# Exponents of the decays in the first stage: differences of running sums brought by a transfer, in place of two matmuls a chunk

## The reference

```python
weights = jnp.where(dist_matrix < CUTOFF, sens, 0.0)      # x = x + weights @ (norm(x) @ W + B)
...
dt = jax.nn.softplus(dt + dt_bias)
A = -jnp.exp(A_log)
dA = jnp.einsum('bclh,h->bhcl', dtc, A)
A_cum = jnp.cumsum(dA, axis=-1)
Lmat = jnp.exp(segsum(dA))                 # exp(cs[l] - cs[s]) for l >= s, else 0
Y_diag = jnp.einsum('bcln,bcsn,bhcls,bcshp->bclhp', Cc, Bc, Lmat, xdt)
decay_states = jnp.exp(A_cum[..., -1:] - A_cum)
states = jnp.einsum('bcln,bhcl,bclhp->bchpn', Bc, decay_states, xdt)
Y_off = jnp.einsum('bcln,bchpn,bhcl->bclhp', Cc, prevs, jnp.exp(A_cum))
Y = (Y_diag + Y_off + xh * D[:, None]).reshape(Bsz, L, D_INNER)
```

## Time and profile before

| what | us |
|---|---|
| median of 3 runs (2483.21 to 2485.96) | 2484.01 |
| the profiled execution | 2485.07 |
| its span, first to last instruction | 2483.2 |
| TensorE matmuls busy | 2268.9 |
| VectorE busy | 1940.7 |
| ScalarE busy | 1493.7 |
| GpSimd busy | 1173.4 |

### The profile page before, as it was taken

The page is one execution under the profiler, slowest core; times in us unless marked ns, Lnnn a source line. Parts: engine busy times, 40 slices in busy tenths (PEclk is TensorE's granted clock), DMA queues, the critical chain, the costliest instruction groups (busy, mean ns, idle before and its releaser), DMA issues.

```text
span 2483.2 us, 26160 instructions
## 1 busy us (share of the span) xinstructions
PE 2268.9 (91%) x8964; PEld 1414.8 (57%) x8964; DVE 1940.7 (78%) x2207; ACT 1493.7 (60%) x2208; POOL 1173.4 (47%) x906
## 2 busy tenths in 40 slices
PE   7998999999999999999899999999999997765998
PEld 4444555555555545545766676666666663433886
DVE  5677878787878776422899899999999898896765
ACT  4676666666667563324575756667675756663444
POOL 2102222223131314311987888888787888791000
PEclk9999999999999999999999999999999998687999
DMA  5232222222222222133323232332323221113121
GB/s 206 94 109 82 70 101 76 93 68 94 68 94 78 84 93 77 59 97 110 111 86 119 96 109 94 103 111 94 119 95 111 94 77 35 43 51 109 36 76 43
DMA packets 111445, 221.15 MB, mean 89 GB/s; under 512 B 7586, under 2 KB 65186, under 8 KB 110930
## 3 DMA queue, kind: packets, MB, share of 16 engines
q1 hardware_dynamic: 107106, 204.00, 25.4%
q0 software_dynamic: 3664, 14.45, 1.6%
q10 hardware_dynamic: 544, 1.05, 0.1%
HBM read 199.28 MB, written 20.19 MB: 88 GB/s over the span
## 4 chain that ended last, share of the span: by engine, by line
PE 42%; DVE 24%; issue 12%; POOL 12%; ACT 9%; DMA 0%; DVEq 0%; POOLq 0%; SPq 0%; ACTq 0%
PE ps L629 9%; POOL dB L2230 8%; DVE h L1431 5%; DVE wgt L1106 4%; PE ps L671 3%; DVE wgt L1099 3%; PE ps L798 2%; PE ps L920 2%; DVE acc L1403 2%; ACT ps L1618 2%; ACT th L1618 2%; POOL acc L2213 2%; PE ps L653 2%; PE ps L733 2%; POOL du L2226 2%
## 5 line engine op out<-in xcount | busy, mean ns | idle before, releaser
L2230 POOL TENSOR_TENSOR dB<-du,bc 128x512 f32<-128x512 f32 x512 | 656.2, 1299 | 92.2 <-DVE h L1431 88.7
L1431 DVE TENSOR_TENSOR_SCAN h<-ps,hst,dB 128x512 f32<-128x512 f32 x512 | 643.6, 1272 | 46.2 <-ACT ps L1618 35.2
L1618 ACT ACTIVATE ps<-dt,cols 128x512 f32<-128x512 f32 x512 | 351.4, 687 | 270.1 <-DVE h L1431 268.1
L629 PE MATMUL ps<-wgt,msg 128*128 128x512 f32 x1024 | 499.1, 596 | 15.1 <-DVE wgt L1106 13.6
L671 PE MATMUL ps<-raw,msg 128*128 128x256 f32 x1792 | 452.8, 389 | 0.9 <-ACT hb L1618 0.9
L920 PE MATMUL ps<-consts,h 128*128 128x128 f32 x2048 | 336.9, 292 | 97.7 <-DVE acc L1403 52.5
L920 PEld LDWEIGHTS ps<-consts,h 128*128 128x128 f32 x2048 | 257.5, 149 | 271.1 <-DVE acc L1403 110.3
L671 PEld LDWEIGHTS ps<-raw,msg 128*128 128x128 f32 x1792 | 331.8, 196 | 74.0 <-issue 39.3
L629 PEld LDWEIGHTS ps<-wgt,msg 128*128 128x128 f32 x1024 | 187.2, 191 | 219.6 <-issue 191.7
L1618 ACT ACTIVATE wgt<-wgt 128x1024 f32<-128x1024 f32 x256 | 258.4, 1049 | 56.1 <-DVE wgt L1099 54.5
L2213 POOL TENSOR_TENSOR acc<-acc,part 128x512 f32<-128x512 f32 x160 | 210.2, 1314 | 80.7 <-ACT part L1618 77.0
(11 more groups left out here) (320 smaller groups left out, 3559.0 us busy)
## 6 DMA issues: line engine op xcount, KB each, us to landing
raw<-in_adjT SPq DMA_DIRECT2D x256, 512.0 KB, 3.6
bc<-tmp_bc SPq DMA_DIRECT2D x64, 512.0 KB, 4.7
xb<-in_xT POOLq DMA_DIRECT2D x8, 512.0 KB, 4.1
tmp_x<-xb POOLq DMA_DIRECT2D x8, 512.0 KB, 3.1
x<-tmp_x SPq DMA_DIRECT2D x8, 512.0 KB, 4.8
tmp_x<-x SPq DMA_DIRECT2D x8, 512.0 KB, 3.6
raw<-tmp_xn SPq DMA_DIRECT2D x8, 512.0 KB, 4.0
tmp_xn<-x SPq DMA_DIRECT2D x7, 512.0 KB, 3.6
```

The source lines that it names most:

```text
L629: x = e.matmul(P[d][:, :], msg[:, j, d * 128:(d + 1) * 128], wgt[g % NW][:, l, :], start=j == 0, stop=j == NJ - 1)
L1431: e.tensor_tensor_scan(hr[n % 3][:, m, :], PS[4 + k % 2].t[:, :], dBr[k % 4][:, :], hst[:, n % 16, m:m + 1], ALU.mult, ALU.add).then_inc(S ...
L1618: return e.activation(out, in_, func, bias=bias, scale=scale)
L2230: e.tensor_tensor(dBr[k % 4][:, :], du[:, m, :], bcr[i % 3][:, n % 2, :], ALU.mult).then_inc(S("dB"), 1)
```

## The change

Running sums cs of dA now come once a block for all four chunks. They get a place in the ring of pre, behind z of the first tile: the three small matmuls that stood at the start of ssd, and a fourth, of dA as weights with tri, that gives the sums turned, 32 rows (chunk and head) of 128. ScalarE copies both out, to `sums_a` (two buffers) and `turned`; ecd is made from `sums_a`. GpSimd's queue stores `turned` to scratch memory, and one transfer a chunk (`load_sums`) brings the chunk's 8 rows to all 128 partitions, straight into E, which has three buffers. GpSimd subtracts the sums of the row's own position and takes the minimum with 0 (above the diagonal cs[l] - cs[s] is positive; cbm is 0 there), and ScalarE takes one exponential over 1024 in place. The load for the next chunk is issued behind the minimum of this one, the first of a block in step 38 of pre. rdA and its two matmuls are gone, and the rings are counted anew. The four steps of a chunk's inner part stay four.

Around it a few semaphores are joined (hst0 and zero1 with zero, A1exp with A1, sum0 with sum, so that the two sums over x3 at the end of a block of the second layer no longer wait for each other).

```diff
-        rdA = sb(cA, "rdA", [128, 8, 128])
-        E = [sb(cA, f"E{i}", [128, 8, 128]) for i in range(2)]
+        sums_a = [sb(cA, f"sums{i}", [128, 3, 4, 8]) for i in range(2)]
+        turned_a = sb(cA, "turned", [32, 128])
+        E = [sb(cA, f"E{i}", [128, 8, 128]) for i in range(3)]
...
-        pre_ring, ssd_ring = Ring(PS[2:4], 12 * NB), Ring(PS[4:8], 41 * NB)
+        pre_ring, ssd_ring = Ring(PS[2:4], 13 * NB), Ring(PS[4:8], 32 * NB)
...
+        def sums_use(ib):
+            return pre_use(ib, 5)
...
+                    if m == 0:
+
+                        b, dA = sums_use(ib), sms[p][:, 3, :]
+                        w.wait_ge(S("dA"), ib + 1)
+                        w.wait_ge(b.evac, b.n - 1)
+                        for k, x in enumerate((tri, trig, one)):
+                            e.matmul(b.ps[:, 32 * k:32 * k + 32], x, dA, start=True, stop=True)
+                        e.matmul(b.ps[0:32, 128:256], dA, tri, start=True, stop=True).then_inc(b.full, 1)
...
-                    yield from (None, None)
-                    for k in range(2):
-                        b = inner_use(ib, s, 2 + k)
-                        w.wait_ge(S("rdA"), 4 * ib + s + 1)
-                        w.wait_ge(b.evac, b.n - 1)
-                        e.matmul(b.ps[:, :], trig, rdA[:, 4 * k:4 * k + 4, :].rearrange("p h l -> p (h l)"),
-                                 start=True, stop=True).then_inc(b.full, 1)
-                        yield
+                    yield from [None] * 4
...
-                    xd, bn, Es, xdec = xdt[s % 2], bns[s % 2], E[s % 2], xdecs[s % 2]
+                    xd, bn, Es, xdec = xdt[s % 2], bns[s % 2], E[(4 * ib + s) % 3], xdecs[s % 2]
...
-                b = ssd_use(ib, 0)
-                w.wait_ge(S("dA"), ib + 1)
-                w.wait_ge(b.evac, b.n - 1)
-                for k, m in enumerate((tri, trig, one)):
-                    i = e.matmul(b.ps[:, 32 * k:32 * k + 32], m, dA, start=True, stop=True)
-                i.then_inc(b.full, 1)
...
-                    yield from (None, None)
+                    yield
+                    if m == 1:
+                        c = sums_use(ib)
+                        w.wait_ge(c.full, c.n)
+                        w.wait_ge(S("cut"), 8 * (ib - 1))
+                        w.wait_ge(S("d_turned"), 16 * ib)
+                        act(sums_a[p][:, :, :, :].rearrange("p a c h -> p (a c h)"), c.ps[:, 0:96], ACT.Identity).then_inc(S("sums_a"), 1)
+                        act(turned_a[:, :], c.ps[0:32, 128:256], ACT.Identity).then_inc(c.evac, 1)
+                    yield
...
-                    for k in range(2):
-                        b = inner_use(ib, s, 2 + k)
-                        w.wait_ge(b.full, b.n)
-                        if c >= 2:
-                            old = outer_use((c - 2) // 4, (c - 2) % 4, 2)
-                            w.wait_ge(old.full, old.n)
-                        act(E[s % 2][:, 4 * k:4 * k + 4, :].rearrange("p h l -> p (h l)"), b.ps[:, :], ACT.Exp).then_inc(b.evac, 1)
-                        yield
+                    x = E[c % 3][:, :, :].rearrange("p h l -> p (h l)")
+                    w.wait_ge(S("cut"), 2 * c + 2)
+                    act(x, x, ACT.Exp).then_inc(S("E"), 1)
+                    yield from (None, None)
...
-                b = ssd_use(ib, 0)
-                w.wait_ge(b.full, b.n)
+                w.wait_ge(S("sums_a"), ib + 1)
                 w.wait_ge(S("xdec"), 4 * ib)
                 w.wait_ge(S("hd"), 4 * ib)
                 if ib:
                     w.wait_ge(outer_use(ib - 1, 3, 0).evac, outer_use(ib - 1, 3, 0).n)
-                act(ecd[:, :, :, :].rearrange("p a c h -> p (a c h)"), b.ps[:, 0:96], ACT.Exp).then_inc(b.evac, 1)
+                act(ecd[:, :, :, :], sums_a[p][:, :, :, :], ACT.Exp).then_inc(S("ecd"), 1)
...
+            def load_sums(c):
+
+                if c >= 3:
+                    old = outer_use((c - 3) // 4, (c - 3) % 4, 2)
+                    w.wait_ge(old.full, old.n)
+                src = t["bc"][c // 4][2 * (c % 4):2 * (c % 4) + 2, :].rearrange("(o n) (a l) -> o (n a) l", o=1, l=128)
+                e.dma_start(E[c % 3][:, :, :], src.broadcast_to([128, 8, 128])).then_inc(S(f"d_E{c % 3}"), 16)
+
             def pre_a(ib):
-                yield from [None] * (NPA - 1)
+                yield from [None] * 24
+                b = sums_use(ib)
+                w.wait_ge(b.evac, b.n)
+                e.dma_start(t["bc"][ib][0:8, :].rearrange("n (a l) -> (n a) l", l=128), turned_a[:, :]).then_inc(S("d_turned"), 16)
+                yield from [None] * 14
+                w.wait_ge(S("d_turned"), 16 * (ib + 1))
+                load_sums(4 * ib)
+                yield from [None] * (NPA - 1 - 24 - 14)
...
-                    w.wait_ge(S("dA"), ib + 1)
-                    if c:
-                        old = inner_use((c - 1) // 4, (c - 1) % 4, 3)
-                        w.wait_ge(old.full, old.n)
-                    e.tensor_tensor(rdA[:, :, :], tri[:, None, :].broadcast_to([128, 8, 128]),
-                                    dA[:, 8 * s:8 * s + 8, None].broadcast_to([128, 8, 128]), ALU.mult).then_inc(S("rdA"), 1)
+
+                    x = E[c % 3][:, :, :]
+                    w.wait_ge(S("sums_a"), ib + 1)
+                    w.wait_ge(S(f"d_E{c % 3}"), 16 * (c // 3 + 1))
+                    e.tensor_tensor(x, x, sums_a[p][:, 0, s, :, None].broadcast_to([128, 8, 128]), ALU.subtract).then_inc(S("cut"), 1)
+                    w.wait_ge(S("cut"), 2 * c + 1)
+                    e.tensor_scalar(x, x, 0.0, None, ALU.min).then_inc(S("cut"), 1)
+                    if s < 3:
+                        load_sums(c + 1)
                     yield
                     w.wait_ge(X.evac, X.n)
-                    w.wait_ge(ssd_use(ib, 0).evac, ssd_use(ib, 0).n)
+                    w.wait_ge(S("ecd"), ib + 1)
                     if c >= 2:
                         old = outer_use((c - 2) // 4, (c - 2) % 4, 1)
                         w.wait_ge(old.full, old.n)
                     e.tensor_tensor(heads(xdec[:, :]), heads(xd[:, :]), ecd[:, 1, s, :, None].broadcast_to([128, 8, 64]),
                                     ALU.mult).then_inc(S("xdec"), 1)
                     yield from (None, None)
-                    for i in (2, 3, 1):
-                        w.wait_ge(inner_use(ib, s, i).evac, inner_use(ib, s, i).n)
-                    e.tensor_tensor(E[s % 2][:, :, :], E[s % 2][:, :, :], cbm[:, None, :].broadcast_to([128, 8, 128]),
+                    w.wait_ge(S("E"), c + 1)
+                    w.wait_ge(inner_use(ib, s, 1).evac, inner_use(ib, s, 1).n)
...
```

89 lines of the change are left out of this document (44 added, 45 removed).

## The result

The changed kernel takes 2501.69 us (median of 4 runs, 2497.99 to 2503.18); the kernel before took 2484.23 beside it. The ratio is 1.0067, 95% interval 1.0050 to 1.0085: it is slower by 17 us, where 2456 had been predicted. The profiled execution took 2497.99 us, its span is 2496.1.

The account below looks back on a forecast made before the run. TensorE, then VectorE, then TensorE was taken to bound blocks 0 to 5, and TensorE blocks 6 and 7. Gains of 17 + 7 + 4.5 - 0.3 = 28 us from 2484.01 gave 2456; range (8 in 10) 2429 to 2479.

Parts of the forecast that it names:

- What bounds the kernel: First stage: blocks 0 to 5 bound by TensorE, then VectorE (496 to 540 us in block 2), then TensorE.
- Matmuls removed: 64 matmuls go; on the chain 4.3 us in each of blocks 0 to 5, 6.6 in block 6, 7.1 in block 7.
- What the longer GpSimd time does to VectorE: 1.7 us more GpSimd reading a chunk holds VectorE up; 1.5 us lost a block, between 0 and 3.4.
- The minimum: GpSimd's new one-input instruction in each chunk; taken as 1.5 us, between 1.1 and 2.36.
- Block 7: GpSimd's chunk of 8.8 us becomes the bound instead of 10.3; 1.5 us gained in three chunks, 4.5 in all.
- Block 6: 6.6 us of matmuls and 3.8 of rdA, against GpSimd's chunk longer by 2.5 three times; 7 us gained.
- Sums moved, transfer, ScalarE: Moved sums taken as 0 in VectorE's part, 0.3 us ahead of block 0; transfers landing in 4.7 us and ScalarE cost nothing.
- What would show it: Signs: blocks 1 to 5 at 116 to 118.5 us, VectorE busy 1 to 4 us more, TensorE idle 5 us a block.
- rival D: Slower: GpSimd's two added instructions hold VectorE four times a block, 6.8 us against 4.3; 2493 us; chance 0.14.
- A: TensorE's work decides after all; all 55 us less 8 x 0.3 go, blocks near 113.7 us; 2431; chance 0.10.
- B: VectorE takes most back: nothing gained in blocks 0 to 5, 11 us in 6 and 7; 2473; 0.18 with C.
- C: Loads into E land late, at 8 us; 2.5 us a block lost and GpSimd waits in block 7; 2477; 0.18 with B.

Follow-up runs that it names:

- e5: e4 with GpSimd waiting, ahead of each of a chunk's instructions, for the end of its previous one; 2456.02 us.
- e13: The changed kernel without the minimum (addition for subtraction), with GpSimd pauses ahead of a chunk's instructions and one ahead of the next load's issue; 2458.0 us.
- e7: The kernel before, with the same GpSimd pauses as e5; 2480.74 us.
- e4: The changed kernel with GpSimd writing dA times tri straight into E; no loads into E, no minimum, no such matmuls; 2482.06 us.
- e17: The whole changed kernel with GpSimd pauses ahead of every instruction of a chunk and one more ahead of the next load's issue; 2491.8 us.
- e6: The changed kernel with GpSimd's pauses as in e5; 2485.76 us.
- e14: e1 with one wait more: GpSimd waits for the end of its addition before issuing the next load; 2465.0 us.
- e16: The whole changed kernel with one wait more a chunk: GpSimd waits for the end of its minimum before issuing the next load; 2498.1 us.
- e10: e8 with three constant matmuls ahead of TensorE's wait for sq; 2468.37 us.
- e18: e8 with one GpSimd pause more, ahead of the next load's issue; 2467.6 us.
- e8: The changed kernel with the minimum moved to ScalarE as Relu ahead of the exponential, and GpSimd's pauses as in e5; 2468.00 us.
- e1: The changed kernel without its minimum, the subtraction made an addition; 2499.83 us.

## Why the prediction was wrong

It was wrong in sign and out of its range: 2456 against 2501.69. By its own steps:

*What bounds the kernel*: right for blocks 0 to 5. VectorE's part of the block and its clashes with GpSimd set the time; the matmuls on the chain counted, the others did not.

*Matmuls removed*: right in size where nothing else intervenes. e5 and e13 have steady blocks of 116.3 and 116.4 us, 4.0 less than before (forecast 4.3), and end at 2456.0 and 2458.0. That the number predicted is also e5's time is luck in its parts. From the profiled executions, blocks 0 to 5 gain 22.4 us in e5 (forecast 17, hold-up taken off), block 6 loses 5.0 (forecast 7 gained), block 7 gains 8.6 (forecast 4.5), and 2.8 come from behind the stage (forecast nothing). Some of it is the worth of the pauses themselves, 3.5 us in the kernel before (e7).

*What the longer GpSimd time does to VectorE*: the step that failed, and in its direction. It priced added reading time (1.7 us a chunk) and let it go to 0 if "the earlier product of chunk 0 (no wait for two exponentials of PSUM) moves the clash away". That earlier product is the damage: the wait for the exponentials was VectorE's way in. 1.5 us a block were taken; e4 against e5 shows 23.5 / 5 = 4.7 us a block with no added GpSimd time at all (0.8 of it the pauses give the kernel before too, e7). With the minimum in place, the pauses give back 10 to 16 us of the run (after against e17 and e6).

*The minimum*: mechanism right, term mis-sized. 1.5 us (to 2.36) was taken from the memset and from E by cbm, on the ground that one input is read; it takes 2.95 in the median and 2.76 at the least. Its price on the run is 33 to 34 us (e14 to e16, e13 to e17). The sum held for it only its part in the 1.5 us of hold-up a block and in GpSimd's chunk in blocks 6 and 7.

*Block 7*: the bound was rightly named, GpSimd's chunk; with 3.0 in place of 1.5 for the minimum 8.8 becomes 10.3, and 10.0 was measured. The block gained 1.4 us instead of 4.5. Without the minimum a chunk takes 8.0 to 8.1 us (e13, e5).

*Block 6*: 7 us gained were forecast, 10.5 were lost, and even e5, the best kernel, loses 5.0. That is a failure of its own, beside a slip: the terms given, 6.6 + 3.8 - 3 x 2.5, make 2.9 and not 7. The sum took L733's share of the chain (8.1%) as time to be gained. What the rows show in its place is waiting: TensorE idles 3.5 us in this block before, 10.1 in e5 and 13.5 after. The granted clock of the block is 1.00 before, 0.94 in e5 and 0.89 after, and with nine matmuls' records fewer TensorE is busy 75.9 us in e5 and 78.0 after, against 77.1. The stretch in e5, and TensorE's waits in it:

```profile
919.60:1005.60 86.00, 75.88 (x284) 42.33 (x283) 50.72 (x67) 29.41 (x46) 28.13 (x19) 0.94 0.20 67
```

```profile
PE ps L586 <- DVE sq L1149: 4.4, 1, 4.4
PE ps L755 <- DVE hs L1231: 3.1, 1, 3.1
```

Before, the waits for the same two were 0.8 us and none; after, 7.2 and 4.2. No run separates that level from the waits in block 6 (e10's three matmuls took 2.1 us off it, 88.1 to 86.0, but e18 without them is 1.5 below e8 too), so the split stays open.

*Sums moved, transfer, ScalarE*: for the transfers the forecast of no cost holds within 2 us, since e13 has the loads and one pause more than e5 and stands 2.0 us above it. The moved sums, the fourth matmul and ScalarE's copies are in e5 too, and no run takes them out; blocks that are 4.0 us shorter where 4.3 were forecast leave them little room.

*What would show it* named VectorE's busy time, up by 1 to 4 us for the forecast and above 102 for rival D. It was 100.1, between the two. TensorE's idle was to be 5 us a block; in block 2 it is 123.1 - 113.2 = 9.9.

*Rivals.* A is out: e5's blocks take 116.3 us, not 113.7. B had VectorE take back the gain of blocks 0 to 5, which it did and more: blocks 1 to 5 are 1.2 us longer each. C is out: GpSimd waited 3.1 us for loads in all. D was right in sign and, at 2493, 9 us off. Its mechanism is half right: GpSimd's instructions back to back hold VectorE for far longer than one of them lasts, and the minimum's length does cost in every block (3.8 us in each of blocks 1 to 5) once VectorE is let in. But it placed the harm in the two added instructions, four times a block, and argued against itself that only two of four rdA stood beside the chain. The long hold is in one place a block, between chunks 0 and 1, and it comes with e4 too, where nothing is added. The Trainium skill, "SBUF — State Buffer", section "Who interferes with whom", says that whichever of the two was issued first holds the other for the whole instruction. The trace agrees that the loser waits out whole instructions (10.12 us for a pair of 2.35), but not that the first start on record wins: in the earlier trace rows L1106 starts at 471.18 and rdA at 471.67, and L1106 is the one that waits. What the wait costs in a row without pauses is shown by e1 and e14 and not by that rule.

The account of the 17.5 us, each term from a pair of runs: the kernel before gains 3.5 from pauses (before to e7); from there the matmuls' removal gains 24.7 (e7 to e5, with everything of the change but loads and minimum); the loads and one pause more cost 2.0 (e5 to e13), the minimum 33.8 (e13 to e17), and taking the pauses away again 9.9 (e17 to after). In sum -3.5 - 24.7 + 2.0 + 33.8 + 9.9 = +17.5. The terms depend on their order: without pauses the minimum is worth 2 (e1 to after) and the matmuls 2 (before to e4).

## What to carry to other kernels

When a change makes an engine's wait go away, ask who used the time of that wait: here VectorE's held instructions got in while GpSimd waited for the exponentials. Where GpSimd and VectorE both read SBUF all the time, try to let GpSimd wait for the end of its own previous instruction at a place where it has time; it costs 0.1 to 0.3 us and was worth 26 us in the kernel with the matmuls alone, 28 in the one with Relu, 35 for a single wait without the minimum. Measure each place: one more such pause cost 6 us in e17. An operation that no row of the trace shows should be measured by itself before it goes into a loop of 32, and an instruction of one input isn't cheaper than one of two for that reason.
